# Product-key experts: the 16 products of inner values and expert weights in each step move from VectorE to GpSimd

## The reference, cut to what matters

```python
xn = _rmsnorm(x, norm_w)                       # x is the layer-normalised h
q = (xn @ w_q.T).reshape(b, t, H, 2, DK)       # H = 8
sim1 = jnp.einsum('bthd,hkd->bthk', q[..., 0, :], keys[:, :, 0, :])   # 64 keys
sim2 = jnp.einsum('bthd,hkd->bthk', q[..., 1, :], keys[:, :, 1, :])
s1, i1 = jax.lax.top_k(sim1, K)                # K = 8
s2, i2 = jax.lax.top_k(sim2, K)
all_sc = (s1[..., :, None] + s2[..., None, :]).reshape(b, t, H, K * K)
fs, pk = jax.lax.top_k(all_sc, K)
fi = jnp.take_along_axis(all_idx, pk, axis=-1) # one of 64 * 64 = 4096 experts
hidden = jax.nn.gelu(jnp.einsum('btd,bthkd->bthk', xn, expert_down[fi]), approximate=False)
hidden = hidden * jax.nn.relu(fs)
return jnp.einsum('bthk,bthkd->btd', hidden, expert_up[fi])
```

## Time and profile before

| | before |
|---|---|
| median of 3 runs | 5304.43 us (5295.95 to 5305.81) |
| the profiled execution | 5299.59 us |
| its span in the profile | 5297.9 us |
| PE busy | 4556.0 us (86%) |
| DVE busy | 3690.1 us (70%) |
| ACT busy | 2142.8 us (40%) |
| POOL busy | 2509.7 us (47%) |
| L3191, the products | 256 on VectorE, from 4143.0 to 5273.2 |
| L3139 on GpSimd | 240, 433.8 us |

### The profile page before, as it was taken

How to read it: one execution, slowest core, us unless ns; L and a number is a source line. 1 busy time by engine, 2 the same in 40 slices (tenths; PEclk the granted TensorE clock), 3 DMA queues, 4 the chain that set the end, 5 groups by cost and what they waited for, 6 DMA issues and landing times. The chain is left out here.

```text
span 5297.9 us, 65263 instructions
## 1 busy us (share of the span) xinstructions
PE 4556.0 (86%) x22344; PEld 2899.1 (55%) x22344; DVE 3690.1 (70%) x7355; ACT 2142.8 (40%) x4025; POOL 2509.7 (47%) x1494
## 2 busy tenths in 40 slices
PE   7888599768888888888885999896998899999999
PEld 4555267533333333333332546793445788888888
DVE  4764222268889888988987323214885999999997
ACT  3654011135555555555553223233663232233322
POOL 3441400279999999999995000000221443334333
PEclk8998799879899999999987999897998899999999
DMA  2003123322222222222221000571002000000000
GB/s 71 1 1 110 59 69 121 114 68 71 70 68 71 67 71 67 71 67 71 68 70 52 0 6 1 222 275 37 1 1 84 3 5 5 5 3 5 5 5 5
DMA packets 153112, 287.22 MB, mean 54 GB/s; under 512 B 24441, under 2 KB 135024, under 8 KB 144206
## 3 DMA queue, kind: packets, MB, share of 16 engines
q1 hardware_dynamic: 144926, 263.59, 15.2%
q0 software_dynamic: 6656, 14.04, 0.8%
q10 hardware_dynamic: 1200, 5.42, 0.3%
HBM read 252.33 MB, written 33.42 MB: 54 GB/s over the span
## 5 line engine op out<-in xcount | busy, mean ns | idle before, releaser
L1509 PE MATMUL ssm_ps<-ssm_hc,net_ident 128*128 128x452 f32 x2048 | 961.8, 596 | 190.9 <-DVE ssm_hc L1765 105.9
L1691 POOL TENSOR_TENSOR ssm_dBu<-ssm_du,ssm_bc 128x904 f32<-128x904 f32 x512 | 1064.6, 2100 | 3.2 <-POOL ssm_du L1709 1.7
L1610 ACT ACTIVATE ssm_ps<-ssm_step,ssm_decay 128x448 f32<-128x448 f32 x1024 | 647.6, 636 | 645.9 <-DVE ssm_ps L1755 435.9
L1509 PEld LDWEIGHTS ssm_ps<-ssm_hc,net_ident 128*128 128x128 f32 x2048 | 392.5, 204 | 726.2 <-issue 347.3
L1755 DVE TENSOR_TENSOR_SCAN ssm_ps<-ssm_ps,ssm_dBu 128x452 f32<-128x452 f32 x512 | 565.1, 1104 | 131.6 <-POOL ssm_dBu L1691 45.2
L1755 DVE TENSOR_TENSOR_SCAN ssm_hs<-ssm_ps,ssm_dBu 128x452 f32<-128x452 f32 x512 | 551.4, 1077 | 41.4 <-ACT ssm_ps L1610 37.0
L1702 POOL TENSOR_TENSOR ssm_hc<-ssm_hs,ssm_bc 128x904 f32<-128x904 f32 x256 | 537.8, 2101 | 74.4 <-DVE ssm_hs L1755 74.4
L3139 POOL TENSOR_TENSOR peer_hot_parts<-peer_hot_cols,peer_parts 128x1024 bf16<-128x1024 bf16 (+1 forms) x240 | 433.8, 1810 | 127.1 <-DVE peer_hot_cols L3157 114.2
L2995 PE MATMUL peer_ps<-peer_xn,peer_down 128*128 128x226 f32 x2048 | 447.4, 365 | 0.0
L3064 PE MATMUL peer_ps<-peer_hid,peer_up 128*128 128x226 f32 x2048 | 398.2, 354 | 1.6 <-DVE peer_hid L3191 1.6
L3064 PEld LDWEIGHTS peer_ps<-peer_hid,peer_up 128*128 128x128 f32 x2048 | 388.9, 190 | 6.5 <-issue 2.2
(11 more groups left out here) (425 smaller groups left out, 8059.5 us busy)
## 6 DMA issues: line engine op xcount, KB each, us to landing
ssm_bc<-ssm_rows SPq DMA_DIRECT2D x256, 452.0 KB, 3.6
ex_w<-in_l_ffn_w SPq DMA_DIRECT2D x64, 1024.0 KB, 6.6
moe_w_gu<-in_moe_gate_up SPq DMA_DIRECT2D x16, 704.0 KB
slots_in<-rt_zeros SPq DMA_DIRECT2D x17, 640.0 KB, 8.6
moe_rows_in<-slots_in SPq DMA_DIRECT2D x16, 512.0 KB
slots_out<-xp_rows_out SPq DMA_DIRECT2D x16, 512.0 KB
moe_w_dn<-in_moe_down SPq DMA_DIRECT2D x16, 384.0 KB
peer_down<-in_peer_down_t SPq DMA_DIRECT2D x1, 4096.0 KB, 17.9
```

The lines of the kernel that those rows point to most:

```text
L1509: nc.tensor.matmul(Y_BANK[j][:, 0:GT], c["ident"][:, :], hc[:, q % 2, j, :], start=False, stop=(n == S - 1))\
L1610: nc.scalar.activation(rows(dA(i % 2))[:, :, lo:lo + N - 1], rows(step[hf.d][:, j, :])[:, :, lo:lo + N - 1], ACT.Exp, scale=decay[hf.d][:, ...
L1691: nc.gpsimd.tensor_tensor(dBu[:, q % 2, j:j + 2, :], du[hf.d][:, j:j + 2, :], bc[:, q % RING, 0:1, :].to_broadcast([P, 2, GT]), ALU.mult). ...
```

## The change

The loop of 16 products is taken out of VectorE's program, where it stood between the centring and the scale of the normalisation, and put at the end of each step of GpSimd's program, behind the last chunk of L3139. The two waits and the semaphore that each product raises go with it; the operation, its tiles and its order are the same.

```diff
                                 .then_inc(s["cols_done"], 1)
+                        pool.wait_ge(s["gelu_done"], (k + 1) * HU)
+                        pool.wait_ge(s["evac_done"], (k + 1) * NC)
+                        for i in range(HU):
+                            block_ = hid[:, i * J:(i + 1) * J, :]
+                            nc.gpsimd.tensor_tensor(block_, block_, weight[:, i * J:(i + 1) * J, :, :].rearrange("p j b n -> p j (b n)"),
+                                                    ALU.mult).then_inc(s["wgt_done"], 1)
 
                 @block.vector
                 def _(dve):
...
                         if afters[k] is not None:
                             norm.vector_centre(nc, dve, h[:, :, afters[k]], k + 3)
-                        dve.wait_ge(s["gelu_done"], (k + 1) * HU)
-                        dve.wait_ge(s["evac_done"], (k + 1) * NC)
-                        for i in range(HU):
-                            block_ = hid[:, i * J:(i + 1) * J, :]
-                            nc.vector.tensor_tensor(block_, block_, weight[:, i * J:(i + 1) * J, :, :].rearrange("p j b n -> p j (b n)"),
-                                                    ALU.mult).then_inc(s["wgt_done"], 1)
                         if afters[k] is not None:
                             norm.vector_scale(nc, dve, k + 3)
```

## The result

| | before | after |
|---|---|---|
| median | 5304.97 us (20 runs, 5289.45 to 5310.49) | 5311.63 us (20 runs, 5306.9 to 5317.36) |
| profiled span | 5297.9 us | 5310.3 us |
| DVE busy | 3690.1 us | 3569.0 us |
| POOL busy | 2509.7 us | 2807.3 us |

The ratio is 1.0015 with a 95% interval of 1.0009 to 1.0022: about 8 us slower (5 to 12). VectorE has 121 us less work, and the kernel is no faster for it. A second series of runs on another chip gave 1.0014 (1.0005 to 1.0023); its trace shows the same steps (the first and the fourth of 14 at 74.98 and 74.95 us, the others at 75.18 to 75.22) and the same 110.1 us from the last similarities to the end.

A forecast was written before the change was run, and what follows sets the result against it. Bound: TensorE, running without a pause and level with VectorE's codes, in steps of 74.95 us. Terms 8.0 - 0.5 + 3.9 = +11.4 us on 5299.59 give 5311.0; with the median 4.8 higher, 5316 us, range 5302 to 5332.

The forecast's parts named there:

- A: Forecast case: VectorE loses at the scale and nearly nothing at the pair sums; 5316 us (5310 to 5320), chance 0.42.
- the race: At the scale: GpSimd's ninth product starts 0.08 us before the scale arrives, making the scale 0.52 us late.
- the last step: Up-projection's first half follows GpSimd's products from the first and ends later: +3.9 us.
- The products covered a wait: VectorE before the scale: the scale also needs the reciprocal root, so removing the products wins 0.39 us a step, not 8.7.
- the slack of the codes: Between VectorE's last codes and TensorE's turning of them: 0.05 us; VectorE later by more moves the whole step.
- the term of 8.0 us: Steps k = 0 to 13: 0.52 at the scale + 0.10 at the pair sums - 0.05 slack, times 14.
- The credit of 0.5 us in k = 14: Step without scale or second moment, where VectorE is later than TensorE: removing the products gains 0.5 us, once.
- case C: Rival: VectorE is first at the scale and the lock costs no time, only the tail remains; 5308 us, chance 0.26.
- The clock of the last step: Up-projection's first half: if gaps between products held TensorE at half rate, +10.6 us instead of 3.9; left unknown.
- Case B: Rival: the pair sums too wait a whole product, 1.1 us more a step; 5331 us, chance 0.18.
- Case D: Rival: GpSimd becomes the bound, a product taking 1.24 us or more; 5335 us, chance 0.08.
- Case E: Rival: codes, not TensorE's hidden matmuls, release the step, winning 0.39 us 14 times, last step free; 5298 us, chance 0.06.

The follow-up runs named there:

- The scan with the pair sums first: Changed kernel with the scale reading PSUM, plus one to seven small memsets on GpSimd ahead of the products, more from step to step; 5248.48 us (one run).
- The scan: Changed kernel plus one to seven small memsets on GpSimd ahead of the products, one more from every second step on; 5238.4 us (one run).
- the kernel with the earlier codes: Changed kernel with last step's products on VectorE, first batch row's search before the scale, codes turned inside the up-projection; 5174.52 us, ratio 0.9895.

## Why the prediction was right, and where it was off

**The direction and the waits held.** The forecast case was A: VectorE loses the race at the scale, little at the pair sums, TensorE starves only in the last step. The trace shows each: the scale printed 1.65 us (forecast 1.5), the series 18.46 (18.4), the loads of the turn wait 0.55 (0.5), the last step loses 4.0 (3.9). Three variants take these waits away one by one: without the second SBUF inputs, or with the series 0.14 us later, the steps are back at 74.95 us, and with the last step's products on VectorE its 4.0 us are back. The forecast 5316 us lies inside the measured runs, 4 us above their median, and the range 5302 to 5332 holds it. By the bound of 0.2% the measured 0.15% is in "within", to which 0.46 was given, and not in "slower" (0.51).

**The products covered a wait.** Shown by the kernel without products: 0.9999.

**The mis-sized term is the slack of the codes.** The prediction gave 0.19 - 0.14 = 0.05 us. Codes were late by 0.68 us (their end lies 36.31 us behind the similarities, before 35.63), as against 0.62 forecast, but the step grew by 0.27 to 0.29 only, so the slack was 0.40. Two things were overlooked. The hand-over from VectorE to TensorE takes 0.06 us here (4709.87 to 4709.93); the prediction's 0.14 was read where TensorE came out of a pause of 1.62 us. And before, the turn's loads were issued at 4702.85 behind hidden matmuls that still ran: ScalarE could copy the result only 1.02 us behind the codes' end at 4702.66, and now it does 0.61 us behind it (4710.48 against 4709.87). The copy in the kernel before:

```profile
4703.68 0.26 ACT L3077 ACTIVATE peer_parts<-peer_ps 128x113 bf16<-128x113 f32 x1
```

Where TensorE waits for the codes, the copy comes 0.41 us sooner behind them. The scan with the pair sums first bears out the size of the slack: its steps whose codes ended up to 35.97 us behind the similarities lasted 74.95 or 74.96 us, and those with 36.08, 36.14 and 36.19 lasted 75.00, 75.06 and 75.10. With 0.40 for 0.05, and the measured 0.68 us in 12 steps instead of 0.62 in 14, the term of 8.0 us would have been 12 x 0.28 = 3.4, where 3.3 was measured.

**The credit of 0.5 us in k = 14** was nothing: from its similarities to the first product of the last step it is 73.47 us (5200.15 to 5273.62) against 73.44 before (5191.71 to 5265.15). The same slack explains it: before, TensorE waited for the codes there and passed them on quickly; now the codes are early and queue behind its own matmuls.

**The two errors offset each other in part.** 3.3 - 0 + 4.0 = 7.3, where 8.0 - 0.5 + 3.9 = 11.4 was forecast.

**The race went the forecast way in part by luck.** The forecast had the scale arrive 8.84 us behind the start of the series (4675.86 - 4667.02), 0.08 behind the ninth product's start, and held that VectorE would be first if it arrived before that start. In the trace it arrives 8.76 us behind (4682.37 - 4673.61), and the ninth product is this one:

```profile
4682.39 1.14 POOL L3147 TENSOR_TENSOR peer_hid<-peer_hid,peer_weight 128x452 f32<-128x452 f32 x1
```

The scale was there 0.02 us earlier and still waited for the whole of it. By the forecast's own rule this would have been case C, with nothing lost in the steps. The scan shows where the edge lies: at 8.70 us VectorE went ahead at once, at 8.76 it lost. The phase was forecast 0.08 us too late and the edge too late as well, and the two errors cancel. In the fourth step of the changed kernel GpSimd started its series 0.28 us later (why is open; the repeat and the variants show it too), the scale came 8.47 us behind it and printed 0.83 us, and that step lasted 74.95: case C's outcome in one step of the same run.

**The clock of the last step**, which the prediction left open at up to 10.6 us, cost nothing more. TensorE at first kept behind the products:

```profile
5273.00:5280.00 7.00, 5.10 (x14) 4.59 (x15) 0.00 (x0) 0.47 (x2) 6.38 (x6) 0.59 0.00 0
5280.00:5285.00 5.00, 5.00 (x25) 4.85 (x24) 0.00 (x0) 0.00 (x0) 5.00 (x6) 0.90 0.00 0
5285.00:5290.00 5.00, 4.81 (x21) 3.17 (x19) 0.00 (x0) 0.00 (x0) 5.00 (x5) 1.00 0.00 0
```

The granted clock is 0.59 in the first 7 us, 0.90 in the next 5 and 1.00 from 5285 on, though TensorE waits 0.34 to 0.42 us in each block there. TensorE caught up with GpSimd at about 5285.5 and waited for six products, so the last product, and not the clock, set the end of the half.

**Case B was priced too low.** It had one further product, 1.1 us. Where the pair sums are the first to meet the series they can wait for all that is left of it, up to 3.4 us; its condition, phases off by 0.1 us, was not the right one either. It did not occur in the changed kernel, where the scale, 6.9 us ahead, had pushed the series back and so set the phase: the pair sums printed 0.73 to 0.75 us in every step.

**Case D** did not come: a product alone printed 1140 ns, as L488 had the earlier trace rows, and in place on `hid` costs nothing more. **Case E** is out: without the products the codes ended 0.42 us earlier (35.21 for 35.63) and the step stayed at 74.95 us, so TensorE was not held by the codes.

## What to carry to other kernels

Ask of work on a full engine what it covers: when the engine's next instruction has an input that comes no earlier, the work is free, and moving it away paid here only together with an order that used the gap. A slack read as a difference of issue times is too small where the later instruction queues behind others; follow it to the first instruction of the next engine. And count the moved work's neighbours: the instructions of VectorE with two SBUF inputs, and the last round, where the pipeline that hid the slower engine has run out.

## What the runs showed of the hardware

GpSimd's product and a VectorE instruction with two SBUF inputs exclude one another: the scale printed up to 1.65 us for 0.62, the product that ran beside it 1.53 for 1.14, and with one input in PSUM the scale printed 0.62 at the same place. The wait ends 0.12 to 0.14 us before the printed end of the running product. The Trainium skill (SBUF — State Buffer, "Summary: rules for kernel authors") says that when VectorE has two SBUF inputs and GpSimd reads SBUF, the second one to issue is blocked until the first finishes. The scan agrees where VectorE meets a running product, with waits of 0.01 to 0.35 us that follow the phase one for one. At the edge the printed starts do not tell who comes first: the scale that starts 0.02 us ahead of a product waited 1.03 us for it.

Unexpected, and not what that rule says, was that a blocked VectorE instruction need not be next. The pair sums waited through the whole rest of a back-to-back series, up to 3.4 us or three products and the rest of one, in 5 of 14 steps of the scan and 3 of 14 steps of the variant with the scale in PSUM, with GpSimd not delayed at all. The scale of these steps never waited for more than one product (at most 1.06 us), and neither did the pair sums in the kernel with the earlier codes, where they were also the first to meet the series, 7.6 to 8.8 us behind its start (0.67 to 1.64 us printed in 14 steps). What decides this is open: scale and pair sums differ in partitions (113 against 128), in their access patterns and in what runs before them, and none of that was tried alone.
